# Single gathers paced two at a time, sixteen more looked-up blocks, and side work dealt out in smaller portions

## The reference, cut to what matters

```python
e = stack([tbl_f[ids[:, f]] for f in range(40)], axis=1)     # (2048, 40, 32)
z = einsum('bke,kef,bkf->bk', e[:, I], W, e[:, J])           # 780 pairs
h = concatenate([z, dense_ctx], axis=1)
h = maximum(h @ W_top1 + b_top1, 0)                          # 796 -> 512
h = maximum(h @ W_top2 + b_top2, 0)                          # 512 -> 256
y = h @ W_top3                                               # 256 -> 1
```

## Time and profile before

| | us |
|---|---|
| runs (3) | 657.39, 658.92, 661.26 |
| median | 658.92 |
| span of the profiled execution | 861.5 |
| PE busy in it | 747.6 (87%) |
| DVE busy in it | 540.2 (63%) |
| POOL busy in it | 402.1 (47%) |

### The profile page before, as it was taken

The page is one execution under the profiler, slowest core; times in us unless marked ns, Lnnn a source line. Parts: engine busy times, 40 slices in busy tenths (PEclk is TensorE's granted clock), DMA queues, the critical chain, the costliest instruction groups (busy, mean ns, idle before and its releaser), DMA issues.

```text
span 861.5 us, 11435 instructions
## 1 busy us (share of the span) xinstructions
PE 747.6 (87%) x4928; PEld 222.9 (26%) x4928; DVE 540.2 (63%) x513; ACT 241.3 (28%) x181; POOL 402.1 (47%) x423
## 2 busy tenths in 40 slices
PE   4768886898889799998899999799988979998998
PEld 1212221222222122222222222222222222222333
DVE  6666665686557566574656658665656665775840
ACT  3524643756123234434302233400000000000002
POOL 6735463454526356446445645454645645453000
PEclk9979997998979889899998889999999989998999
DMA  8712202011201202010111010100110110100100
GB/s 264 254 32 70 70 11 60 17 34 46 72 26 29 69 8 63 18 32 12 46 46 47 11 45 11 45 11 8 48 45 11 48 45 11 46 11 7 37 1 1
DMA packets 26963, 38.08 MB, mean 44 GB/s; under 512 B 9552, under 2 KB 16352, under 8 KB 26784
## 3 DMA queue, kind: packets, MB, share of 16 engines
q1 hardware_dynamic: 13568, 30.49, 10.8%
q0 software_dynamic: 13312, 6.84, 5.3%
q10 hardware_dynamic: 32, 0.01, 0.0%
HBM read 22.36 MB, written 0.01 MB: 26 GB/s over the span
## 4 chain that ended last, share of the span: by engine, by line
PE 63%; another core or an unknown queue 16%; DVE 9%; ACT 7%; issue 3%; DMA 1%; DVEq 0%; SPq 0%; ACTq 0%
PE tps L729 24%; PE zps L751 17%; PE mlp_ps L802 12%; DVE prods L707 8%; PE mlp_ps L782 7%; PE tps L802 3%; ACT hot L561 3%; ACT hot L564 3%; DMA zs<-in_hot_table 1%; ACT zs L530 0%; ACT parts L553 0%; PE zps L738 0%; ACT eT L579 0%; DVE hot L650 0%
## 5 line engine op out<-in xcount | busy, mean ns | idle before, releaser
L707 DVE TENSOR_TENSOR prods<-tps,eT 128x1024 f32<-128x1024 f32 x400 | 469.6, 1218 | 264.6 <-PE tps L729 141.4
L514 POOL DMA_INDIRECT rows<-in_table,idx x416 | 401.5, 965 | 381.7 <-DVE prods L707 257.4
L729 PE MATMUL tps<-eT,weights 32*128 32x512 f32 x1600 | 302.0, 677 | 62.8 <-DVE prods L707 42.3
L751 PE MATMUL zps<-prods,select 128*32 128x512 f32 x1600 | 224.7, 652 | 13.5 <-ACT zs L530 10.6
L729 PEld LDWEIGHTS tps<-eT,weights 32*128 32x128 f32 x1600 | 87.1, 194 | 231.2 <-DVE prods L707 113.7
L782 PE MATMUL mlp_ps<-hot,parts 128*32 128x512 bf16 x1344 | 113.3, 421 | 27.8 <-issue 10.8
L561 ACT ACTIVATE hot<-ids,minus_code 128x2048 bf16<-128x2048 int16 x47 | 93.8, 1995 | 67.3 <-PE mlp_ps L782 46.6
L802 PE MATMUL mlp_ps<-zs,w1s 128*128 128x512 f32 x182 | 94.3, 649 | 6.8 <-ACT eT L579 6.8
L564 ACT ACTIVATE hot<-hot,ones 128x2048 bf16<-128x2048 bf16 x47 | 94.1, 2002 | 1.5
L751 PEld LDWEIGHTS zps<-prods,select 128*32 128x32 f32 x1600 | 38.7, 112 | 178.4 <-issue 112.0
L530 ACT ACTIVATE zs<-zps 128x512 f32<-128x512 f32 x28 | 16.7, 597 | 211.5 <-PE zps L751 123.3
(11 more groups left out here) (29 smaller groups left out, 50.1 us busy)
## 6 DMA issues: line engine op xcount, KB each, us to landing
eT<-eT SPq DMA_DIRECT2D x38, 192.0 KB
ids<-in_hot_ids SPq DMA_DIRECT2D x14, 512.0 KB
rows<-in_table,idx POOLq DMA_INDIRECT x416
eT<-eT SPq DMA_DIRECT2D x38, 128.0 KB
eT<-eT SPq DMA_DIRECT2D x38, 64.0 KB
zs<-in_hot_table SPq DMA_DIRECT2D x4, 512.0 KB, 7.9
w1s<-in_w SPq DMA_DIRECT2D x1, 1792.0 KB
weights<-in_wt SPq DMA_DIRECT2D x1, 960.0 KB
```

What stands on the lines that cost most here:

```text
L514: pool.indirect_dma_start(rows[:, k % ROW_SLOTS, m * EMB:(m + 1) * EMB], None, table, bass.IndirectOffsetOnAxis(ap=idx[:, g, t, m:m + 1], ...
L707: dve.tensor_tensor(prods[:, at % PROD_SLOTS, 2 * half:2 * half + 2, :], tps[:, (2 * at + half) % PAIR_BANKS, :, :], tiles, ALU.mult).then ...
L729: last = pe.matmul(tps[:, (2 * at + half) % PAIR_BANKS, bank, :], weights[part, n, :], eT[part, slot_of(t, g), :], start=True, stop=True)
L751: last = pe.matmul(zps[EMB * r:EMB * (r + 1), :], select[:, off:off + EMB], prods[:, at % PROD_SLOTS, bank, :], start=kt < KT - 1 and slot ...
```

## The change

Six things are changed.

1. `HOT_COUNT` goes from (4, 4, 4, 2) to (4, 4, 4, 4): groups 2 and 3 of chunk 3 are looked up (16 units more, beside chunk 2's quads) and no longer gathered (384 gathers, 24 transpositions).
2. Seven one-hot slots for four. The memory is that of the ring in which POOL writes its DMA descriptors: `dynamic_dma_scratch_size=4096`, 12 KB a partition less than before, and a slot is 4 KB.
3. With the smaller ring, POOL waits ahead of every gather for the landing of the gather two before (`IN_FLIGHT`, `landed`), and the landings are counted by two semaphores a slot, one for even and one for odd gathers. DVE waits for both.
4. `PARTS_AT` is every gather: each waits for its own count of products or units.
5. Layer tiles are cut 3, 2, 2 (7 steps) and 2, 2 (4 steps) in chunks 1 and 2 alike, and a hot group takes two cycles, two units beside each quad. Chunks 1 and 2 each have 17 cycles with steps and 8 with four units.
6. One-hot tiles for chunks 2 and 3 are made 1 to 8 quads ahead by unit, in the cycles with steps but for units 0 and 7; odd units by DVE, even ones by ACT.

```diff
-HOT_COUNT = (4, 4, 4, 2)
+HOT_COUNT = (4, 4, 4, 4)
-HOT_SLOTS = 4
+HOT_SLOTS, FIRST_UNITS = 7, 4
...
         else:
-            starts = list(range(0, len(tile) - 1, 2)) if t > 1 else [0, 4] if at < 2 else [0]
+            starts = [0] + list(range(len(tile) % 2 + 2, len(tile) - 1, 2))
...
             if batch[-1][2] == 0 and batch[-1][3] < len(hots) and batch[-1][4] == KT - 1:
-                blocks += [(hots[batch[-1][3]], u) for u in range(0, UNITS, 2)]
+                blocks += [(hots[batch[-1][3]], u) for u in range(0, UNITS, FIRST_UNITS)]
...
                 h, u = block
-                sides[at].append(("hot", h, u))
-                sides[at + 1].append(("hot", h, u + 1))
+                for unit in range(u, u + FIRST_UNITS):
+                    sides[at + (unit - u) // 2].append(("hot", h, unit))
...
-    return [g > 1 and u == 5, ((h - HOT_COUNT[0]) * UNITS + u) % 3 > 0, u % 2 == 1][min(t, 2)]
+    return [g > 1 and u == 5, ((h - HOT_COUNT[0]) * UNITS + u) % 3 > 0, u % 2 == 0][min(t, 2)]
...
-MADE_AHEAD = 4
+MADE_AHEAD = (8, 5, 7, 4, 6, 3, 5, 1)
...
-            MAKES[side_at - MADE_AHEAD].append(item[1:])
+            MAKES[side_at - MADE_AHEAD[item[2]]].append(item[1:])
...
-PARTS_AT = [0, 6, 11]
+PARTS_AT = list(range(GATHERS))
+IN_FLIGHT = 2
...
+def landed(k, m):
+
+    i = k * GATHERS + m
+    return i // GATHERS % ROW_SLOTS, i % IN_FLIGHT, 16 * ((i // GATHERS // ROW_SLOTS * GATHERS + i % GATHERS) // IN_FLIGHT + 1)
...
                     if m in PARTS_AT:
-
+                        if k * GATHERS + m >= IN_FLIGHT:
+                            slot, turn, count = landed(k, m - IN_FLIGHT)
+                            pool.wait_ge(rows_gathered[slot][turn], count)
...
-                    ).then_inc(rows_gathered[k % ROW_SLOTS], 16)
+                    ).then_inc(rows_gathered[k % ROW_SLOTS][m % IN_FLIGHT], 16)
...
-                dve.wait_ge(rows_gathered[k % ROW_SLOTS], (k // ROW_SLOTS + 1) * (16 * GATHERS))
+                for turn in range(IN_FLIGHT):
+                    dve.wait_ge(rows_gathered[k % ROW_SLOTS][turn], (k // ROW_SLOTS + 1) * (16 * GATHERS // IN_FLIGHT))
...
-    nc = bacc.Bacc("TRN2", target_bir_lowering=False, num_devices=1)
+    nc = bacc.Bacc("TRN2", target_bir_lowering=False, num_devices=1, dynamic_dma_scratch_size=4096)
```

More of the change, by code:

```diff
@@ L153, in plan_sides @@
         for u in range(UNITS):
-            sides[at + u // HOT_SLOTS].append(("hot", h, u))
+            sides[at + u // FIRST_UNITS].append(("hot", h, u))
     own = HOT_COUNT[0]
@@ L215, in by_scalar @@
     t, g = HOTS[h]
-    return [g > 1 and u == 5, ((h - HOT_COUNT[0]) * UNITS + u) % 3 > 0, u % 2 == 1][min(t, 2)]
+    return [g > 1 and u == 5, ((h - HOT_COUNT[0]) * UNITS + u) % 3 > 0, u % 2 == 0][min(t, 2)]
 def made_until(h, u, scalar):
     return sum(by_scalar(h_, u_) == scalar for h_ in range(len(HOTS)) for u_ in range(UNITS) if (h_, u_) <= (h, u))
-MADE_AHEAD = 4
+MADE_AHEAD = (8, 5, 7, 4, 6, 3, 5, 1)
 MAKES = {at: [] for at in range(TOTAL)}
-MAKES[0] = [(2, u) for u in range(HOT_SLOTS, UNITS)]
+MAKES[0] = [(2, u) for u in range(FIRST_UNITS, UNITS)]
 for unit in range(UNITS):
-    MAKES[3 if by_scalar(3, unit) else 1 + unit // HOT_SLOTS].append((3, unit))
+    MAKES[3 if by_scalar(3, unit) else 1 + unit // FIRST_UNITS].append((3, unit))
 for side_at, items in SIDES.items():
@@ L373, in build @@
         ids_based = sem("ids_based")
-        rows_gathered = [sem(f"rows_gathered{s}") for s in range(ROW_SLOTS)]
+        rows_gathered = [[sem(f"rows_gathered{s}_{turn}") for turn in range(IN_FLIGHT)] for s in range(ROW_SLOTS)]
         w_loaded = [sem(f"w_loaded{s}") for s in range(len(LOADS))]
@@ L681, in _ @@
             rest(2, 0)
-            for u in range(HOT_SLOTS):
+            for u in range(FIRST_UNITS):
                 make_unit(2, u)
```

## The result

The changed kernel takes 697.62 us (median of 4 runs, 695.90 to 700.89) where the kernel before takes 658.15; the ratio is 1.060 [1.056, 1.064]. Forecast were 670.3 us and a range of 655 to 684: the sign was right, the size was not, and the time lies 13.6 us above the range. The profiled execution has a span of 696.0 us beside a run of 697.8, so here profile and runs tell the same story, unlike before.

The account below looks back on a forecast made before the run. The prediction took PE to bound the loop, with DVE a close second. To the median of 658.9 us it added 10.4 for units, -4 for portions and 5 for two gathers under way: 670.3 us, range 655 to 684.

Parts of the forecast that it names:

- PE bounds the loop, cycles by their content: Whole loop: PE sets the pace, 9 parts in 10; two bare quads 4.19 us, a step 0.86, a unit 0.65.
- L782 near 129 us busy: Sign expected in the profile after: source line L782 with 1536 matmuls, near 129 us busy.
- Sixteen units +10.4: Chunk 2: sixteen more units at 0.65 us of PE each, on the path, +10.4 us; their one-hot tiles hidden.
- a close second: Loop: DVE needs 5.79 us for two quads with product, one-hot tile and transposition, against PE's 5.43.
- Portions -4: Mainly chunk 1: recut steps and units relieve cycles where DVE or a switch held PE; -4 us, between 0 and 7 gained.
- A mark per gather 0: POOL's queue: only POOL waits for marks, so 0 us on the path if gathers come in time.
- 32 gathers fewer 0: Fewer gathers and two transpositions fewer: they spare the path between 0 and 0.8 us, taken as 0.
- Two under way +5, at most 16: Chunk 0: the landing wait makes rows late after a slow start, POOL at 1.25 to 1.40 us a gather; +5 us, 0 to 16.
- the prediction's own sum: Chunk 0 lateness at quad 40: start lag 14, plus growth up to 8, plus landing 2.4, less slack 7.3, less loop slip 6.
- The 202.6 us as the profile's own load: Profiled span beyond the timed runs: PE's creeping while gathers run, read as profiling load; at most 10 us left open as real.
- Bursts were real: Rival: PE's creeping in gather bursts is partly in timed runs, so even spacing removes it; 650 us, chance 0.13.
- gathers bound chunk 0: Rival: in chunk 0 POOL takes 1.40 us or more a gather and the loop doesn't slip; 682 us, up to 690, chance 0.12.

Follow-up runs that it names:

- Four_ring8_hot2_e: Changed kernel with four gathers under way, 8 KB ring, six one-hot slots and the old HOT_COUNT (4, 4, 4, 2): 658.44 us, ratio 1.0006 to the kernel before.
- two_wait_e: Kernel before plus only the landing wait of two (each gather waits for the gather two before): 711.68 us against 657.69, ratio 1.081.
- after_e: The changed kernel unaltered, timed again beside the kernel before on a quick chip: 695.72 us against 659.20, ratio 1.054.
- four_ring8_c: Changed kernel with four gathers under way, 8 KB ring and six one-hot slots, on a slower chip: 758.5 us against 850.7 for the kernel before, ratio 0.892.
- after_again: The changed kernel unaltered, timed once more on another chip of the quick kind: 697.21 us against 659.23 for the kernel before, ratio 1.057.

## Why the prediction failed

- **PE bounds the loop, cycles by their content**: right. Cycles of 5.91, 6.77, 6.72 and 5.37 us stand in after as they were worked out, and with 36 steps for 34 a chunk the sum for chunk 1 is met. Bare cycles are 4.54 to 4.58, not 4.19. The sign "L782 near 129 us busy" missed: it is 102.5, since 129 was scaled from the trace of before, where PE's records are longer.
- **Sixteen units +10.4**: 7.7 (6 to 9). The unit was sized right (0.65), but the cycles that it displaces were costed at 4.19 where DVE's products hold them at 4.58. I had named DVE "a close second" and had a one-step cycle of 5.36 against 5.05 in the earlier trace rows; the same excess was to be charged to bare cycles.
- **Portions -4**: 0. Four_ring8_hot2_e, with them, stands 0.75 us above before. It was the lower end of my bound. The 7-step cycles of the earlier trace rows do vanish, but on the quick chips they had no excess (10.16), and the 1.2 us that chunk 1 gains is lost again in chunk 2.
- **A mark per gather 0**: right on the quick chips as far as is known, for it was timed there only with the portions.
- **32 gathers fewer 0**: right only with room for gathers. Beside the landing wait they are worth 25 us (chunk 3 of two_wait_e against after_e).
- **Two under way +5, at most 16**: 29.6. This step broke the forecast, with the mechanism right (start late, chunk 0 can't catch up, DVE at the transposition, PE behind it) and both its inputs too small. The start: gather 16 at 46.3 us, 21 after it was due rather than 14. The pace: 1.57 us each, not 1.25 to 1.40, so over the 79 gathers to the end of the sixth group the lag grows by 79 x 0.27 = 21, not 8. By the prediction's own sum, 21 + 21 + 2.4 - 7.3 - 6 = 31. That this is near 29.6 is in part luck, for with four under way gather 16 comes at 33.0, 8 us after it was due, and nothing waits, and the 6 was never measured. Against that run, gather 16 is 13.3 us later and gather 95, the last of the sixth group, 33.1 (170.1 for 137.1): some 13 are of the start and some 20 of the pace. The 1.25 came from one gather whose data landed 1.9 us after its start, with an estimate of 0.3 to 0.7 for the way to the next start. The ordinary gather of after has nearly that (2.4 to the landing and 0.26 on, 1.33 each), which already doesn't catch up; the late ones, up to 5.0, had no term, and the bound 1.40 had no row at all. Both gathers of the start, 4.6 and 5.6 us, spoke for more, and I treated them as the start's affair. The rule of the Trainium skill ("DMA: Bandwidth & Descriptors", section "Anatomy of one DMA — SWDGE (gpsimd) path"; 2.04 us for 16 KB), by which two under way never wait, is below every landing that the trace of after tells, 2.2 us at least; the measurement decides.
- **The 202.6 us as the profile's own load**: wrong in its reason. The runs of 659 us don't have the creeping, as I said, but on other chips all runs of before are as long (median 852), and the profiled execution is no slower than the others of its kernel (four_ring8_c: 759.33 among 756.83 to 762.14). By all signs a profile of one kind of chip stood beside times of the other. The record gives a span and a clock for every run, so it doesn't show what a run without any recording takes. "Bursts were real" had 0.13 and would have been right on those.

Together 0.75 + 7.7 + 29.6 = 38 us; that is a sum of differences of the same medians and proves nothing by itself. Over the kernel before on the same chip the change costs 36.5 us (after_e), 38.0 (after_again) and 39.5 (the result). The "gathers bound chunk 0" rival had the right place; its worst case, 690, was short by the start and the pace.

## What to carry to other kernels

A limit on transfers under way is a pace: landing time over the number allowed. Take the landing time from many gathers, late ones included, and not from a quiet one, and compare the pace with the stretch that wants the most; here one more pair in flight was worth 30 us. When a profile and the times disagree by 30%, ask first whether they are of the same kind of chip. And a change that adds work to the bound engine to spare another is worth what the other's limit is: with four gathers under way sixteen units for 32 gathers cost 6 to 9 us, with two they save 25 in chunk 3, more than they cost.

## What the runs showed of the hardware

- The same program takes 659 us on some chips and 852 on others. Spacing gathers evenly (marks) gives 0.936 of the time there; on the quick chips, together with the portions, it gives 1.0006. On the slower ones a stretch with a gather each 1.5 us or so and no look-ups keeps the quick pace (132.9 us for 132.7).
- A stall of DVE of 6.19 us cost PE 8.45; the granted clock was 0.54 in the 7.5 us after it, and the eight matmuls of the transform took 3.19 us instead of 1.14.
- A gather that overlaps a one-hot tile of DVE holds POOL for 1.07 us in the mean, the others for 0.95 (60 and 324 in after).
- Gathers of 16 KB land 2.4 us after their start in the middle case, and release their second successor 2.5 to 5.2 us after their start in chunk 0, and over 5 beside the first loads; in after the gather of 26.09 waited for that of 17.23, 8.86 us:

```profile
26.09 1.08 POOL L523 DMA_INDIRECT rows<-in_table,idx  x1 [6.02 <-DMA rows<-in_table,idx]
```
